# Layer-norm statistics for the first MoE, taken batch by batch inside the attention

## The reference, cut to what matters

```python
def _layernorm(x, axis=-1, eps=1e-05):
    m = jnp.mean(x, axis=axis, keepdims=True)
    v = jnp.var(x, axis=axis, keepdims=True)
    return (x - m) / jnp.sqrt(v + eps)

x = x + _L0_xattn_ref(_layernorm(x), ctx_2048, wq, wk, wv, wo, ...)   # attention, 16 heads, 4 key groups
x = x + _L0_ffn_ref(_layernorm(x), gate, expert_bias, w1, w2, w3, ...) # MoE, 2 of 8 experts and a shared one
x = x + _L1_xattn_ref(_layernorm(x), ctx_2048, mask)                   # attention to the memory rows
x = x + _L1_ffn_ref(_layernorm(x), router_w, gate_w, up_w, down_w)     # MoE, 1 of 8 experts
```

## Time and profile before

| | |
|---|---|
| median of 3 runs | 3104.29 us (3102.34 to 3104.94) |
| profiled execution, its own time | 3110.86 us |
| its span, first to last instruction | 3109.0 us |
| TensorE clock granted, mean over the span | 0.969 of 2.4 GHz |
| busy share of the span: PE, PEld | 93%, 79% |
| DVE, ACT, POOL | 70%, 65%, 51% |

### The profile page before, as it was taken

One profiled execution on the slowest core, in us unless ns is written; L12 is line 12 of the kernel. 1 busy time (PEld: TensorE's weight loads), 2 busy tenths in 40 slices (PEclk: granted clock), 3 DMA queues, 4 the chain that ended last, 5 costly groups with the idle time before them and its releaser, 6 DMA issues. The chain is left out here.

```text
span 3109.0 us, 61537 instructions
## 1 busy us (share of the span) xinstructions
PE 2893.1 (93%) x18731; PEld 2456.1 (79%) x18731; DVE 2182.6 (70%) x4617; ACT 2027.7 (65%) x5169; POOL 1597.5 (51%) x2081
## 2 busy tenths in 40 slices
PE   5887999899999999999999999999999977599788
PEld 4665888678888888888888888888888864388755
DVE  7995444567777777777777777777777768756544
ACT  5664666667777777777777777777777647656211
POOL 5884333355555555555555555555555444376132
PEclk9998999999999999999999999999999979899799
DMA  4335666610110110110110110110110010254511
GB/s 133 118 112 177 203 203 203 214 55 33 53 46 33 53 46 33 53 46 34 53 46 33 53 46 33 53 46 33 53 46 33 1 46 1 73 166 131 173 39 28
DMA packets 244462, 236.02 MB, mean 76 GB/s; under 512 B 11654, under 2 KB 224527, under 8 KB 244208
## 3 DMA queue, kind: packets, MB, share of 16 engines
q1 hardware_dynamic: 225552, 212.01, 20.8%
q10 hardware_dynamic: 16448, 15.73, 1.7%
q0 software_dynamic: 2208, 5.12, 0.6%
HBM read 148.93 MB, written 84.80 MB: 75 GB/s over the span
## 5 line engine op out<-in xcount | busy, mean ns | idle before, releaser
L952 ACT ACTIVATE pt_hi<-ps_t 128x512 fp32r<-128x512 f32 (+2 forms) x1024 | 570.0, 557 | 415.1 <-PE ps_t L1185 411.8
L1020 DVE TENSOR_REDUCE piece_max<-ps_s 128x1 f32<-128x512 f32 (+2 forms) x1024 | 631.2, 622 | 260.9 <-PE ps_s L1172 232.9
L1046 DVE TENSOR_TENSOR pt_lo<-ps_t,pt_hi 128x512 fp32r<-128x512 f32 (+2 forms) x1024 | 656.0, 641 | 200.5 <-ACT pt_hi L952 184.0
L1116 POOL TENSOR_SCALAR prob<-prob,inv_sum 128x512 f32<-128x512 f32 (+2 forms) x1024 | 637.1, 642 | 282.1 <-DVE inv_sum L1036 282.1
L940 ACT ACTIVATE prob<-ps_s,neg_max 128x512 f32<-128x512 f32 (+2 forms) x1024 | 648.9, 634 | 92.7 <-DVE neg_max L1027 84.1
L1205 PE MATMUL ps_o<-pt_hi,v_hi 128*128 128x256 f32 (+1 forms) x1856 | 595.7, 321 | 0.0
L1185 PE MATMUL ps_t<-ident,prob 128*128 128x128 f32 (+1 forms) x3712 | 572.0, 272 | 1.4 <-DVE pt_lo L1046 1.3
L1207 PE MATMUL ps_o<-pt_hi,v_lo 128*128 128x256 f32 (+1 forms) x1856 | 523.4, 282 | 0.0
L1206 PE MATMUL ps_o<-pt_lo,v_hi 128*128 128x256 f32 (+1 forms) x1856 | 522.2, 281 | 0.0
L1185 PEld LDWEIGHTS ps_t<-ident,prob 128*128 128x128 f32 (+1 forms) x3712 | 456.6, 140 | 60.0 <-issue 1.7
L1167 PE MATMUL ps_s<-k_hi,q_hi 128*128 128x512 f32 (+2 forms) x1024 | 405.2, 396 | 27.8 <-ACT prob L940 19.6
(11 more groups left out here) (267 smaller groups left out, 5619.9 us busy)
## 6 DMA issues: line engine op xcount, KB each, us to landing
v_scratch<-v_out SPq DMA_DIRECT2D x120, 256.0 KB, 2.5
raw_k<-k_scratch SPq DMA_DIRECT2D x32, 960.0 KB
raw_v<-v_scratch SPq DMA_DIRECT2D x32, 960.0 KB
k_scratch<-k_out SPq DMA_DIRECT2D x104, 256.0 KB, 2.4
q_scratch<-out_t SPq DMA_DIRECT2D x64, 256.0 KB, 2.6
raw_q<-q_scratch SPq DMA_DIRECT2D x32, 512.0 KB
c_raw<-in_ctx_t ACTq DMA_DIRECT2D x52, 256.0 KB, 2.8
raw_t<-in_ctx_t SPq DMA_DIRECT2D x24, 512.0 KB, 4.1
```

The costliest lines, as they stand in the source:

```text
L952: nc.scalar.activation(pt_hi[keys, k % RING, cols], ps_t[keys, k % 2, cols], ACT.Copy).then_inc(hi_done, 1)
L1020: nc.vector.tensor_reduce(piece_max[:, n % 2, p:p + 1], ps_s[:, p, lo - p * PC:hi - p * PC], AX.X, ALU.max).then_inc(max_ready, 1)
L1046: nc.vector.tensor_tensor(pt_lo[keys, k % RING, cols], ps_t[keys, k % 2, cols], pt_hi[keys, k % RING, cols].bitcast(F32), ALU.subtract).th ...
L1116: nc.gpsimd.tensor_scalar(prob[:, n % PB, lo:hi], prob[:, n % PB, lo:hi], inv_sum[:, n % PB:n % PB + 1], 1.0, ALU.mult, ALU.mult).then_inc ...
```

## The change

The statistics move from the MoE's block into the attention's. `norm` (the buffer of the statistics, 448 bytes in each partition with its companion, and four semaphores) is allocated in `program` and handed to both stages. In bodies i = 2, 4, ... 14, VectorE gets three more things to do at the end of slot 6: in units 1 and 3 a `bn_stats` of one tile of the batch that is finished, and in unit 5 the two `bn_aggr`. These are 14 `bn_stats` and 14 `bn_aggr`, for tiles 0 to 13. The MoE's VectorE stream now begins with tiles 14 and 15 alone, and makes `xn` of all parts directly behind. GpSimd's stream is the same text; its first three waits (4, 8 and 12 tiles aggregated) are met before the block begins.

```diff
-def attention(nc, q_dram, k_dram, v_dram, x_sb, ident, ident_bf, mask_bf, operands):
+def attention(nc, q_dram, k_dram, v_dram, x_sb, mean_var, norm, ident, ident_bf, mask_bf, operands):
...
+                def row_stats(i, tile):
+                    dve.wait_ge(y_added, YA_CREDIT + i * (BODY_U // 2))
+                    nc.vector.bn_stats(norm[0][:, tile, :], x_sb[:, tile, :]).then_inc(norm[2], 1)
+
+                def row_mean_var(tile):
+                    dve.wait_ge(norm[2], tile + 1)
+                    nc.vector.bn_aggr(mean_var[:, tile, :], norm[0][:, tile, :]).then_inc(norm[3], 1)
...
                             elif s == 6 and u == 0 and positive(i):
                                 add_y(i - 1, BODY_U - 1)
+                            if s == 6 and i >= 2 and i % 2 == 0:
+                                if u in (1, 3):
+                                    row_stats(i, i - 2 + u // 2)
+                                elif u == 5:
+                                    row_mean_var(i - 2)
+                                    row_mean_var(i - 1)
...
 def moe_two_of_eight(nc, x_sb, gate_dram, bias_dram, w1_dram, w3_dram, w2_dram, sw1_dram, sw3_dram, sw2_dram,
-                     mean_var, rstd, half, ident, ident_bf, iota):
+                     mean_var, rstd, half, ident, ident_bf, iota, norm):
...
-        norm = norm_memory(sb, sem, "norm2")
...
-                norm_mean_var(nc, dve, x_sb, mean_var, norm, 0)
+                for t in range(NT - 2, NT):
+                    nc.vector.bn_stats(norm[0][:, t, :], x_sb[:, t, :]).then_inc(norm[2], 1)
+                for t in range(NT - 2, NT):
+                    dve.wait_ge(norm[2], t + 1)
+                    nc.vector.bn_aggr(mean_var[:, t, :], norm[0][:, t, :]).then_inc(norm[3], 1)
                 for part in range(NORM_PARTS):
-                    if part + 1 < NORM_PARTS:
-                        norm_mean_var(nc, dve, x_sb, mean_var, norm, part + 1)
                     dve.wait_ge(norm[-1], part + 1)
...
         mean_var = sb("mean_var", [P, NT, 2])
+        norm = norm_memory(sb, sem, "norm2")
```

More of the change, by code:

```diff
@@ L2585, in program @@
                                 ((ident_bf, ident), (upper_bf, upper), (causal_bf, causal)), (consts_loaded, 48), ones_bf, operands)
-            attention(nc, q_dram, k_dram, v_dram, x_sb, ident, ident_bf, causal_bf, operands)
-        moe_two_of_eight(nc, x_sb, gate, expert_bias, w1, w3, w2, sw1, sw3, sw2, mean_var, rstd, half, ident, ident_bf, iota)
+            attention(nc, q_dram, k_dram, v_dram, x_sb, mean_var, norm, ident, ident_bf, causal_bf, operands)
+        moe_two_of_eight(nc, x_sb, gate, expert_bias, w1, w3, w2, sw1, sw3, sw2, mean_var, rstd, half, ident, ident_bf, iota, norm)
         rows_written = sem("rows_written")
```

## The result

The changed kernel takes 3110.43 us (median of 15 runs, 3106.68 to 3114.87) against 3105.08 for the kernel before (15 runs, 3102.34 to 3107.77). The ratio is 1.0017, with a 95% interval of 1.0009 to 1.0025: slower by 5.3 us, between 2.8 and 7.8. A second set gave 3110.78 against 3105.64, ratio 1.0017 (1.0008 to 1.0026). So it is within 0.2%, and on the slower side of the 3106.1 us that was forecast. The first figure lies 0.07 us inside the upper end of the range, 3110.5, and the second 0.3 us beyond it.

A forecast was written before the change was run, and what follows sets the result against it. TensorE was taken to bound the kernel. A 0.8 us gain at the MoE's head and a 2.6 us price in the attention gave +1.8 us, on 3104.29 a forecast of 3106.1 us; range 3101.5 to 3110.5.

The forecast's parts named there:

- unit 1: Attention, even bodies: a `bn_stats` adds 0.33 us, less slack of 0.12 at ScalarE and 0.10 at TensorE; TensorE loses 0.11.
- the buffers' place: Attention: buffers lying 448 bytes further on were taken to cost nothing.
- The bound: Attention: TensorE, busy 494.98 of 500 us, sets the pace; other work costs only where it makes TensorE wait.
- all is hidden: Rival: later waits in the attention take up the delays, only the MoE head counts; -0.8 us, 3103.5; chance 0.15.
- no slack: Rival: each new attention instruction is paid whole in TensorE's time; +7.0 us, 3111.3; chance 0.10.
- The price of one instruction: Attention, VectorE: a `bn_stats` delays what follows by 0.33 us start to start, as `add_y` does, though that lasts 0.41.
- The rival with whole durations: Attention: new instructions overlap less than `add_y`, slacks as seen; 0.61 us a body, +3.5, 3107.8; chance 0.10.
- Unit 3: Attention, even bodies: a `bn_stats` adds 0.33 us, less slack of 0.07 at ScalarE and none at TensorE; loses 0.26.
- Unit 5: Attention, even bodies: two `bn_aggr` add 0.14 us, under the slack of 0.22; costs nothing.
- The whole loop: Attention: a body loses 0.37 us, seven bodies lose 2.6 us; bounds nothing and 7.8.
- The head: Start of the MoE: `xn` 1.77 us earlier, but TensorE waits for the bias; gain 0.8 us, bounds nothing and 1.8.
- The rival in which it stays up: MoE head: TensorE restarts before the clock falls and the work holds full clock; about 10 us less, 3096; chance 0.05.

The follow-up runs named there:

- experiment 1: Changed kernel with the new attention instructions one slot later, behind the `low` at the end of slot 7: 3106.77 us against 3105.64 before, ratio 1.0003.
- experiment 7: Kernel before with only the statistics' buffer and semaphores allocated early, all statistics still made in the MoE: 3107.53 us against 3105.31 before, ratio 1.0004.
- experiment 2: Changed kernel with each new attention instruction made twice, the first into an unread spare tile: 3113.54 us against 3105.64 before, ratio 1.0026.
- experiment 3: Changed kernel with TensorE's two waits for the next keys moved ahead to slot 5 of units 1 and 5: 3107.12 us against 3106.86 before, ratio 1.0001.
- experiment 4: Changed kernel with TensorE's wait for gate and bias moved behind its first four transposes: 3108.22 us against 3105.31 before, ratio 1.0008.
- experiment 5: Kernel before with only TensorE's wait for gate and bias moved behind its first transposes: 3102.66 us in one execution.
- experiment 6: Changed kernel with new instructions behind slot 7 and the gate and bias wait behind the first transposes: 3104.12 us against 3105.64 before, ratio 0.9995.
- experiment 9: Changed kernel with new instructions behind slot 7, later gate and bias wait, and key waits in slot 5: 3102.76 us against 3106.86 before, ratio 0.9988.

## Why the prediction was right or wrong

*The number.* The absolute time, 3110.43 us, is inside the range by 0.07 us, and that is luck: the second set's is outside, and the difference, 5.3 us, is about three times the 1.8 forecast. The direction, and that it is within 0.2%, came out as forecast. The mechanism was right in the main, with one step wrong in the price (unit 1) and one term put at nothing without a bound (the buffers' place).

*The bound.* Right. TensorE set the pace, and the new work of VectorE cost only through the chain at a unit's end, with the two places and the pair of `bn_aggr` as foreseen. Moved out of that chain, the same instructions cost nothing: the loop of experiment 1 is that of experiment 7, 1843.6 us. The rival "all is hidden" is out, since the three places show in the loop. So is "no slack": unit 1 lost 0.21 of 0.33, since the 0.12 at ScalarE was real.

*The price of one instruction.* 0.33 us from start to start, as taken from `add_y`; measured 0.33, once and twice (experiment 2). The rival with whole durations, by the Trainium skill's page VectorE: DVE Perf Modes, section The DRAIN you can't avoid, is out: the `bn_stats` lasts 0.42 and the next instruction starts 0.33 after it. The same section adds that a next instruction that is not held starts earlier, which the prediction left out and these rows agree with. That rival's +3.5 us lies nearer to what was measured than the forecast does, but for another reason than its own.

*Unit 3.* 0.26 forecast, 0.28 measured. *Unit 5.* Nothing forecast, 0.02 measured.

*Unit 1.* 0.11 forecast, 0.21 measured, and this is the step that failed: the 0.15 us from the accumulator's end to TensorE, against 0.05 in unit 3, was read as "slack 0.10", and the two waits for the next keys were taken "as passed before". They were passed, but they need an instruction of their own, and that instruction carries the wait for the exponential. So 0.10 us (0.09 unrounded: 0.144 against 0.053) lies behind the exponential every time, however late it is. Experiment 2 leaves it unchanged under load, and experiment 3 removes it. Seven times 0.10 is 0.7 us of the miss. With 0.12 at ScalarE as the only slack the prediction's own sum gives 0.33 - 0.12 = 0.21 at unit 1 and 0.14 - 0.12 = 0.02 at unit 5, as measured.

*The whole loop.* 2.6 forecast, 4.4 to 4.7 measured: 3.6 us from the three places (0.51 a body), and 0.8 to 1.1 from units 0 and 4, where the forecast was nothing ("both buffer sets of the attention lie at different places today and I take nothing"). That reason was no bound, and the kernel with the early buffer alone has it too (experiment 7), though it is not shown that the buffers' place makes it.

*The head.* 0.8 us forecast, 0.6 and 0.9 measured in two profiles. The mechanism was right in each part: `xn` 1.85 us earlier (1.77 forecast), the bias as the releaser. In the first profile its landing took 3.0 us after the issue and not 2.7, in the second 2.7. Experiments 4 and 5 show it from both sides. It passed on whole as far as it can be followed: TensorE's first transposes of a group's scaled inputs (L1612 of the kernel before) start 34.19 and 33.92 us after its last attention work, against 34.78 before.

*The clock.* The rival in which it stays up did not come: in the changed kernel it fell in the pause. It had two conditions. The first, that TensorE restarts before the fall, was met in experiments 6 and 9, with a pause of 3.65 us, and not in experiment 4 with the same pause. The second, that the head's work holds the full clock, failed both times: the clock fell 1.6 and 1.1 us behind the restart, with TensorE busy nearly without a break. So the 10 us of that rival did not come there either, but about 0.5 us did. Of the Trainium skill, TensorE: Matmul & The Clock Gate, the rule that idleness takes the full clock away agrees with the falls within the pause; the two falls behind the restart it does not give by itself.

*The sum.* With the measured terms: 3.6 + about 1 - 0.6 to 0.9 = 3.7 to 4.0 us, inside the measured 2.8 to 7.8. The forecast of 1.8 was not. What the medians show beyond 4 us is less than the interval of the comparison, and I have no cause for it. In two experiments loop and head together miss the medians by as much the other way: they give 9.2 us over before in experiment 2, where the medians have 7.9, and 1.7 in experiment 3, where they have 0.3.

## What to carry to other kernels

An engine that is idle a quarter of its time is not free at every point: put extra work behind the instruction that another engine waits for, and not in front of it. Here the same instructions cost 3.6 us in one slot and nothing in the next. Before counting the time between a release and a start as slack, look at what it is made of: in this kernel two waits more on an instruction were a second instruction, and as that one carried the late wait, its 0.1 us was paid every time. And when a producer is moved earlier, look for the wait that was hidden behind it: here a DMA of 4 KB kept half of the gain and more.

## What the runs showed of the hardware

TensorE's scores start 0.05 us after the end of the accumulator's read when that is their only wait, and 0.15 us when two more waits, long met, stand with it. In this kernel that was 31 places in a loop of 1842 us, and moving the two waits three slots ahead took 2.6 us off the loop with the later slot (1843.7 in experiment 6, 1841.1 in experiment 9) and 1.8 with the slot of the change (experiment 3).

A VectorE instruction of 0.41 to 0.42 us (`bn_stats`, `add_y`) let the next one start after 0.33 us; a `bn_aggr` of 0.15 to 0.17 us let it start after 0.07 to 0.09.

The granted clock fell to half while TensorE's records show it busy 0.87 to 1.00 of each microsecond, after a pause of 3.65 us with the clock at full (experiment 6).

The loop repeats from one profiled execution of a build to the next within 0.15 us (1842.5 and 1842.4; 1846.9 and 1847.1), while three builds with the same instructions in the attention differ by up to 2.0 us (1841.6, 1842.4 and 1843.6), in the same two of eight units. A difference of a microsecond between such loops is more than that scatter, and may have nothing to do with the edit in question.
